# Rounds of four steps in a fused attention kernel, with the side tasks behind the products with V

## What is computed

```python
latent_kv = x @ w_kv_down
kv = latent_kv @ w_kv_up
k, v = (kv[..., :HD], kv[..., HD:])
q = (x @ w_q).reshape(Bx, Tx, N_HEAD, HEAD_SIZE)
att = jnp.einsum('bqhd,bkhd->bhqk', q, k) * scale
att = jnp.where(causal, att, -jnp.inf)
att = jax.nn.softmax(att, axis=-1)
y = jnp.einsum('bhqk,bkhd->bqhd', att, v)
return y.reshape(Bx, Tx, HD) @ w_out
```

## Time and profile before

| | us |
|---|---|
| median of 3 runs | 2115.67 |
| lowest, highest | 2113.73, 2116.21 |
| profiled execution, span from first to last instruction | 2113.7 |
| PE busy | 1984.7 (94%) |
| POOL busy | 1425.9 (67%) |
| DVE busy | 1337.2 (63%) |
| ACT busy | 1097.9 (52%) |

### The profile page before, as it was taken

The page is one execution under the profiler, slowest core; times in us unless marked ns, Lnnn a source line. Parts: engine busy times, 40 slices in busy tenths (PEclk is TensorE's granted clock), DMA queues, the critical chain, the costliest instruction groups (busy, mean ns, idle before and its releaser), DMA issues.

```text
span 2113.7 us, 35206 instructions
## 1 busy us (share of the span) xinstructions
PE 1984.7 (94%) x12886; PEld 1240.9 (59%) x12886; DVE 1337.2 (63%) x2728; ACT 1097.9 (52%) x2236; POOL 1425.9 (67%) x812
## 2 busy tenths in 40 slices
PE   8997788999999999999989999999999999999898
PEld 6775454555655555555555655555555555555466
DVE  7786555576656666666665657576756575656443
ACT  5775543455545454545455444545445445444585
POOL 1333225778687878787857687868786878687822
PEclk9998899999999999999999999999999999999999
DMA  3000000000000000000000000000000000000001
GB/s 124 1 1 1 0 7 13 13 19 10 13 18 16 13 19 12 19 10 19 13 12 17 12 20 11 17 12 20 11 18 11 20 11 18 11 14 11 26 26 60
DMA packets 29243, 37.01 MB, mean 18 GB/s; under 512 B 6928, under 2 KB 20368, under 8 KB 29072
## 3 DMA queue, kind: packets, MB, share of 16 engines
q1 hardware_dynamic: 29072, 34.76, 5.4%
HBM read 30.02 MB, written 4.46 MB: 16 GB/s over the span
## 4 chain that ended last, share of the span: by engine, by line
PE 63%; DVE 14%; POOL 12%; ACT 6%; issue 4%; DMA 1%; POOLq 0%; ACTq 0%; SPq 0%; DVEq 0%
PE heads_out L918 16%; POOL acc L1416 10%; PE beside L723 9%; PE scores L723 7%; PE two_heads L874 7%; PE scores L897 4%; PE scores L903 4%; PE scores L899 4%; PE scores L901 4%; DVE part_max L1112 3%; ACT prob L1331 2%; PE two_heads L723 2%; PE beside L929 2%; PE heads_out L723 1%; DVE wQK_lo L1073 1%
## 5 line engine op out<-in xcount | busy, mean ns | idle before, releaser
L1416 POOL TENSOR_TENSOR acc<-acc,prob 128x1024 f32<-128x1024 f32 (+3 forms) x512 | 1017.9, 1988 | 195.4 <-ACT prob L1331 140.1
L1331 ACT ACTIVATE prob<-scores 128x512 f32<-128x512 f32 (+3 forms) x1280 | 579.4, 539 | 649.2 <-PE scores L903 289.0
L1112 DVE TENSOR_REDUCE part_max<-two_heads 128x2 f32<-128x1024 f32 x384 | 469.3, 1222 | 280.5 <-PE two_heads L874 279.7
L918 PE MATMUL heads_out<-prob,V 128*64 128x512 f32 (+3 forms) x2560 | 544.4, 547 | 0.0
L1109 DVE CUSTOM_DVE_ANT_0 two_heads<-two_heads,mask 128x128 f32<-128x128 f32 (+3 forms) x512 | 242.0, 514 | 180.4 <-PE two_heads L874 180.4
L874 PE MATMUL two_heads<-k_hi,q_hi 64*128 64x512 f32 (+3 forms) x1280 | 274.1, 424 | 62.8 <-DVE part_max L1112 30.6
L918 PEld LDWEIGHTS heads_out<-prob,V 128*64 128x64 f32 x2560 | 156.7, 137 | 232.4 <-issue 209.6
L874 PEld LDWEIGHTS two_heads<-k_hi,q_hi 64*128 64x128 f32 x1280 | 120.6, 184 | 256.6 <-issue 133.4
L897 PE MATMUL scores<-q_hi,k_hi 64*128 64x512 f32 (+3 forms) x1280 | 236.1, 364 | 0.8 <-DVE k_lo L1100 0.5
L903 PE MATMUL scores<-neg_max,sel 64*128 64x512 f32 (+3 forms) x1280 | 235.6, 362 | 0.0
L901 PE MATMUL scores<-q_lo,k_hi 64*128 64x512 f32 (+3 forms) x1280 | 235.5, 362 | 0.0
(11 more groups left out here) (301 smaller groups left out, 2898.7 us busy)
## 6 DMA issues: line engine op xcount, KB each, us to landing
rden<-rden_rows SPq DMA_DIRECT2D x128, 128.0 KB, 2.9
X<-u SPq DMA_DIRECT2D x8, 512.0 KB, 8.7
out<-X SPq DMA_DIRECT2D x8, 512.0 KB, 2.9
wQK_raw<-wQuery SPq DMA_DIRECT2D x16, 192.0 KB, 3.1
wO_raw<-wOut SPq DMA_DIRECT2D x16, 128.0 KB, 2.8
wV_raw<-wValue SPq DMA_DIRECT2D x8, 128.0 KB, 2.9
den<-den_rows SPq DMA_DIRECT2D x64, 4.0 KB
rden_rows<-den SPq DMA_DIRECT2D x64, 4.0 KB, 1.3
```

The source lines that it names most:

```text
L918: made = pe.matmul(heads_out[head(h), x0:], V[vn % NVS][:, tt, p % 2, head(h)], prob[step % NPROB][:, h, x0:], start=t == 0, stop=t == TPB ...
L1112: made = ve.reduce_max(part_max[:, t, :, c:c + 1], two_heads[:, :, 0:width], AX.X)
L1331: ac.activation(prob[step % NPROB][:, h, x0:], bank(task, h)[:, x0:], ACT.Exp).then_inc(empty(task, h)[0], 1)
L1416: po.tensor_tensor(total[:, :, x0:], total[:, :, x0:], new[:, :, x0:], ALU.add).then_inc(acc_ok, 1)
```

## The change

A round now has four steps. Its order is: a maximum, the scores of two steps, a maximum (or a piece of weights), `invert`, the scores of the other two steps, the rest of the round's maxima (one in banks 5 and 6, the next in 0 and 1, a third in 2 and 3), then the products with V of these same four steps with `two_parts` behind the second, and behind them `scale_out`, `denominators` and up to four tasks beside, in banks 7, 3, 2 and 1, the fourth only if it is due within eight steps. The table `TILE` sets in which order a unit takes its key tiles: with j = 3, each round takes three full tiles and one diagonal one; with j = 2 one, one and two; with j = 1 two and two; with j = 0 all four are diagonal. The two heads of a step share one wait, one semaphore and one exponential of up to 1024 columns. Due times of values and of the output's tasks move with the rounds. Nothing is computed that was not before.

```diff
+SIDE = [7, 3, 2, 1]
+TILE = [[0, 1, 2, 3], [0, 1, 4, 5, 2, 3, 6, 7], [0, 1, 2, 8, 3, 4, 5, 9, 6, 7, 10, 11], [0, 1, 2, 12, 3, 4, 5, 13, 6, 7, 8, 14, 9, 10, 11, 15]]
...
+def tile_of(idx, t):
+
+    return TILE[UNITS[idx][2]][t]
+
+
+def left_of(idx, t):
+
+    return P * max(0, tile_of(idx, t) - TPB * UNITS[idx][2])
...
         elif kind == "maximum":
-            self.take(task, (5, 6))
+            self.take(task, (self.max_bank, self.max_bank + 1))
         elif kind == "score":
             n = 2 * (self.step_of[task[1:]] % 2)
-            if task[2] >= TPB * UNITS[task[1]][2]:
+            if tile_of(*task[1:]) >= TPB * UNITS[task[1]][2]:
                 self.masked[task[1:]] = len(self.masked) + 1
-            self.take(task, (n,), (n + 1,))
+            self.take(task, (n, n + 1))
...
             _, idx, t = task
-            x0 = P * max(0, t - TPB * UNITS[idx][2])
+            x0 = left_of(idx, t)
...
-                    out.append((max(start[first] + 2 if j else start[first] - LEAD - 8, at + TPB * j - 14), at + TPB * j - 2 + half, ("value", self.value_of(b, p, j), half)))
+                    out.append((start[first] + 4 * (j - 1) if j else start[first] - LEAD - 8, at - 4 + half, ("value", self.value_of(b, p, j), half)))
...
-        ahead = {-14: [("channel_start", "b"), ("mixer_weights", "b"), ("turn_normal", "b", 0)],
-                 -12: [("turn", "b", 0), ("turn_normal", "b", 1)], -10: [("turn", "b", 1), ("mix_tokens", "b", 0)],
-                 -4: [("turn_normal", "b", 2)], 0: [("mix_tokens", "b", 1)]}
+        ahead = {-16: [("channel_start", "b"), ("mixer_weights", "b"), ("turn_normal", "b", 0)],
+                 -12: [("turn", "b", 0), ("turn_normal", "b", 1)], -8: [("turn", "b", 1), ("mix_tokens", "b", 0)],
+                 -4: [("turn_normal", "b", 2), ("mix_tokens", "b", 1)]}
...
-            later.extend([(s + 2, ("denominators", idx)), (s + 6, ("invert", idx)), (s + 8, ("scale_out", idx)), (s + 10, ("two_parts", idx))])
+            later.extend([(s + 4, ("denominators", idx)), (s + 8, ("invert", idx)), (s + 8, ("scale_out", idx)), (s + 12, ("two_parts", idx))])
...
-        for s in range(0, len(steps) + 2, 2):
+        for s in range(0, len(steps), 4):
             self.in_steps = True
-            if s == 2:
-                self.heads_free = self.freed[4]
...
-            goal = min(len(self.maxima), max(urgent, min(s + 2 + LEAD, self.at + 3))) if self.layers_done else urgent
+            goal = min(len(self.maxima), max(urgent, min(s + 4 + LEAD, self.at + 5))) if self.layers_done else urgent
             if self.at < goal:
                 maximum()
-            due("invert")
             for step in steps[s:s + 2]:
                 self.need("score", *step)
+            if not s:
+                self.in_steps = False
+                yield
+                self.in_steps = True
             if self.at < goal:
                 maximum()
             else:
                 chore()
-            filler(10 ** 6)
-            diagonal = not steps[s:s + 2] or any(t >= TPB * UNITS[idx][2] for idx, t in steps[s:s + 2])
-            if not diagonal:
-                self.side_bank = 0
-                filler(s + 8)
-                self.side_bank = 7
-            while self.at < goal - 1:
+            due("invert")
+            for step in steps[s + 2:s + 4]:
+                self.need("score", *step)
+            self.max_bank = 5
+            while self.at < goal:
                 maximum()
-            for idx, t in steps[max(0, s - 2):s]:
+                self.max_bank = (5, 0, 2)[(5, 0, 2).index(self.max_bank) - 2]
+            self.max_bank = 5
+            if not s:
+                self.heads_free = self.freed[4]
+            for idx, t in steps[s:s + 4]:
                 self.need("weigh", idx, t)
                 self.need("accumulate", idx, t)
+                if (idx, t) == steps[s + 1]:
+                    due("two_parts")
                 if t == TPB * (UNITS[idx][2] + 1) - 1:
                     self.need("take_out", idx)
                     output(idx)
-            if self.at < goal:
-                maximum()
-            due("two_parts")
             due("scale_out")
-            if not due("denominators") and diagonal:
-                filler(s + 8)
+            for n, self.side_bank in enumerate(SIDE):
+                if n or not due("denominators"):
+                    filler(10 ** 6 if n < 3 else s + 8)
+            self.side_bank = 7
             if side:
-                self.add_all(side.pop(0))
+                for piece in (side.pop(0), side.pop(0) if side else []):
+                    self.add_all(piece)
             self.add_all(ahead.get(s - len(steps), []))
             self.in_steps = False
             yield
+        s = len(steps)
...
+        def pair_of(task):
+            first = plan.bank[task][0][0][0]
+            return two_heads if first == 5 else scores[:, first:first + 2, :]
...
-                    for h in range(2):
-                        for s, v in free(task, h):
-                            w.wait_ge(s, v)
+                    for s, v in free(task):
+                        w.wait_ge(s, v)
+                    first = plan.bank[task][0][0][0]
...
                     for h in range(2):
-                        pe.matmul(bank(task, h)[:, x0:], k_hi[g][head(h), kc], q_hi[i][head(h), x0:], start=True, stop=False)
+                        pe.matmul(scores[:, first + h, x0:], k_hi[g][head(h), kc], q_hi[i][head(h), x0:], start=True, stop=False)
...
                     for h in range(2):
-                        pe.matmul(bank(task, h)[:, x0:], sel[head(h), :], neg_max[idx % NMAX][head(h), x0:], start=False, stop=True).then_inc(full(task, h)[0], 1)
+                        made = pe.matmul(scores[:, first + h, x0:], sel[head(h), :], neg_max[idx % NMAX][head(h), x0:], start=False, stop=True)
+                    made.then_inc(full(task)[0], 1)
...
-                    if t >= TPB * UNITS[idx][2]:
+                    if task[1:] in plan.masked:
                         w.wait_ge(masked, plan.masked[idx, t])
-                    for h in range(2):
-                        w.wait_ge(*full(task, h))
-                        ac.activation(prob[step % NPROB][:, h, x0:], bank(task, h)[:, x0:], ACT.Exp).then_inc(empty(task, h)[0], 1)
+                    first = plan.bank[task][0][0][0]
+                    w.wait_ge(*full(task))
+                    ac.activation(prob[step % NPROB][:, :, x0:], scores[:, first:first + 2, x0:], ACT.Exp).then_inc(empty(task)[0], 1)
                 elif kind == "take_out":
...
```

More of the change, by code:

```diff
@@ L873, in tensor_program @@
                     for h in range(2):
-                        made = pe.matmul(two_heads[:, h, 0:width], q[head(h), t * P:(t + 1) * P], k[head(h), 0:width], start=True, stop=True)
+                        made = pe.matmul(pair_of(task)[:, h, 0:width], q[head(h), t * P:(t + 1) * P], k[head(h), 0:width], start=True, stop=True)
                     made.then_inc(full(task)[0], 1)
@@ L1297, in scalar_program @@
                     if idx >= NQ:
-                        w.wait_ge(*full(("score", *last_step(idx - NQ)), 1))
+                        w.wait_ge(*full(("score", *last_step(idx - NQ))))
                     ac.activation(q_hi[idx % NQ][:, :], bank(task), ACT.Copy, scale=DH ** -0.5).then_inc(q_hi_ok, 1)
@@ L1303, in scalar_program @@
                     if idx >= NKS:
-                        w.wait_ge(*full(("score", *last_of_pair(idx - NKS)), 1))
+                        w.wait_ge(*full(("score", *last_of_pair(idx - NKS))))
                     ac.activation(k_hi[idx % NKS][:, :], bank(task), ACT.Copy).then_inc(k_hi_ok, 1)
@@ L1314, in scalar_program @@
                     if idx >= NMAX:
-                        w.wait_ge(*full(("score", *last_step(idx - NMAX)), 1))
+                        w.wait_ge(*full(("score", *last_step(idx - NMAX))))
                     ac.activation(neg_max[idx % NMAX][:, :], bank(task), ACT.Copy, scale=-1.0).then_inc(empty(task)[0], 1)
@@ L1402, in gpsimd_program @@
                     step = step_of[idx, t]
-                    x0 = P * max(0, t - TPB * UNITS[idx][2])
+                    x0 = left_of(idx, t)
                     total, new = acc[idx % 2], prob[step % NPROB]
-                    for h in range(2):
-                        w.wait_ge(*empty(("score", idx, t), h))
+                    w.wait_ge(*empty(("score", idx, t)))
                     if t == 1:
```

25 lines of the change are left out of this document (11 added, 14 removed).

## The result

The changed kernel takes 2311.39 us (median of 4 runs, 2307.58 to 2313.4), the kernel before 2114.7 in the same comparison: 1.0925 times as long (95% interval 1.0909 to 1.0940), 197 us more. The forecast was 2207, range 2075 to 2265: the right side, but 91 us in place of 197.

A forecast was written before the change was run, and what follows sets the result against it. PE, 96% busy in the attention stretch, was taken as the bound. 127 + 16 + 28 + 6 - 74 - 12 = +91 us on the 2113.7 span gives 2204.7; with 2.0 for the median, 2207 us, range 2075 to 2265.

The forecast's parts named there:

- The release time: Score banks: free 1.36 us after their score slot ends, from 0.28 latency, 1.02 merged exponential and 0.06 semaphore.
- M4: Last maximum of a round of four, in the banks of S2: waits 0.11 to 0.64 us with j = 3.
- S2: Third score step of a round, reusing the first one's banks: waits 0.11 us, about 1.0 with j = 0.
- 127 + 16 + 6: PE's costs: 127 us waiting for reused score banks, 16 for `invert` delaying limits, 6 for a fifth maximum in bank 2.
- Tasks beside right ahead of the scores: Tasks in banks 7, 3, 2, 1 before the next round's first scores: their evacuations cost 28 us, bounds 0 and 70.
- What was to be won: PE's waits of maxima for DVE reductions and of denominators for their bank: 74 us, nearly all to go.
- Blocks of four products with V: Weighing in fours instead of twos saves a switch of task kind each round: 12 us won, 0 to 22.
- The faster case: Rival: score banks come free in time, release about 0.9 us, 86 us won, about 2060 us; chance 0.20.
- POOL was no bound: Rival: POOL bounds full-width stretches and spreading diagonal tiles frees it, some 2000 us; chance 0.03, within the faster case's.

The follow-up runs named there:

- b_side_first: Kernel before, with the task beside put ahead of the second maximum in rounds whose two tiles are 256 and 128 wide: 2105.8 us, 0.9951 of before.
- a_tiles_in_order: Changed kernel with each unit's key tiles in natural order, so all four diagonal tiles fall in its last round: 2352.6 us, 1.1134 of before.
- a_late_between: Changed kernel with the fourth maximum behind the second product with V and one task beside between the pairs of scores: 2188.14 us, 1.0351 of before.
- a_max_late: Changed kernel with maxima from the fourth of a round on issued behind the second product with V: 2235.35 us, 1.0579 of before.
- a_dve_clear: Changed kernel with the reciprocal and the maxima's pieces of weights moved behind the second pair of scores: 2263.13 us, 1.0712 of before.
- a_keep_clock: Changed kernel with seven useless transposes between third and fourth maximum in rounds with two or more diagonal tiles: 2307.35 us, 1.0920 of before.
- a_three: Changed kernel with late fourth maximum, reciprocal and weights behind the second scores, and one task beside between the pairs of scores: 2243.37 us, 1.0602 of before.

## Why the prediction was right and wrong

*The release time was right.* ACTIVATE by width in the changed kernel (mean ns after the comma):

```profile
L1352 ACT ACTIVATE prob<-scores 128x1024 f32<-128x1024 f32 x436 | 435.8, 1025 | 325.7 <-PE scores L925 247.2 <-DVE scores L1143 69.9 <-POOL acc L1436 6.6
...
L1352 ACT ACTIVATE prob<-scores 128x768 f32<-128x768 f32 x62 | 50.1, 809 | 8.1 <-DVE scores L1143 4.8 <-POOL acc L1436 3.4
...
L1352 ACT ACTIVATE prob<-scores 128x512 f32<-128x512 f32 x61 | 36.5, 598 | 56.9 <-DVE scores L1143 56.8
...
L1352 ACT ACTIVATE prob<-scores 128x256 f32<-128x256 f32 x61 | 23.3, 382 | 4.5 <-DVE scores L1143 2.5 <-POOL acc L1436 1.5
```

1025 ns at 1024 columns, against 1.02 us forecast. In the four rounds of a unit with j = 3, M4 starts 1.35 to 1.47 us after the slot of S2 ends (forecast 1.36) and loses 0.04, 0.34, 0.49 and 0.66 us in the median (forecast 0.11, 0.33, 0.56, 0.64). M4 costs 97 us by the starts, some fifth maxima included, and the scores 52; the forecast had 127 + 16 + 6 for all of them and `invert`. The sum of 149 is met, its inside only in part, and that is luck: M4 in the last round of j = 2 loses 0.35 in place of 0.8, and in the last round of j = 1 it loses 2.4 in place of 0.8 and half a us for `invert`. The prediction counts `invert` on DVE and leaves out `chore`, the piece of weights that rides with each maximum and stands ahead of the same limits, held up by POOL: of a task that is moved, every rider moves with it.

*Tasks beside right ahead of the scores* were forecast at 28 and cost 32.

*What was to be won failed.* "Nearly all go" of 74 us: 45 did, and 29 us of waits for reductions stayed. This is one step that failed; the other is that three costs had no term at all (below). The forecast counts the distance between two maxima on PE; what it leaves out is what DVE has still to do before it can reduce the first one. In the changed kernel that is a piece of the output's weights (`wO_lo`, issued ahead of the round's first maximum) in 14 waits with 17 us, row statistics of a coming layer in 7 more with 6, and the evacuation of a key in 16 with 5. The reciprocal and the limits have under 1 us of it. In the kernel before, more distance did help wherever there was a task to give it (b_side_first); I had read a releaser as the whole cause.

*Three costs had no term in the sum.* The half clock: 33 us more of it than before. The forecast has PE waiting for over 140 us and treats each wait as its length. The query that is made in the last round before its maxima: 26 us. The tasks of the second sequence (`turn_tiles` and `latent`), now one behind the other behind the products with V: some 13 us more by the starts.

*Blocks of four products with V* were forecast at -12. The step from one weigh task to the next is in fact shorter in the block (0.86 us against 0.91 for full width), the step from a maximum into the block costs 0.1 more than the step from a maximum to a score. By the starts that makes -10 to -20 in all, so I let -12 stand.

Together: 149 + 32 + 33 + 26 + 13 - 45 - 12 = 196, and the spans differ by 192.5 (2306.2 and 2113.7). The forecast had 91: of the 105 between them, 29 are what wasn't won, 33, 26 and 13 the terms left out, and 4 the tasks beside. That is closer than it deserves, since the half clock also stretches the distances that the other terms are read from.

*The rivals.* The faster case needed a release of 0.9 us or less in place of 1.36; nothing of it came. POOL was no bound: its share of the chain fell to 1% while PE's waits grew. It isn't out of the picture either, since it holds the pieces of weights on DVE. (That PE's idle rows of the kernel before name POOL nowhere is almost right: there is one wait of 3.3 us before `project`.) Spreading the tiles does help (41 us), by way of DVE and ACT. The forecast's range ended at 2265, since it allowed for a bad case only of the terms it had.

*Open* is what POOL's hold on the pieces of weights is worth by itself, and whether a kernel with rounds of four and a shorter lead of the maxima could match the one before. The best of them stands 3.5% above it.

## What to carry over

When a bank's turn is shortened from a round to two slots, the chain behind it (last product, limit on DVE, exponential, semaphore) has to be set against the slots of PE that follow, width by width; the time of that chain can be read from the old trace to a few per cent. Then go through every engine of that chain for what is queued ahead of the evacuating instruction, riders included, for it is the round where two small things coincide that costs most. Work that is put off comes in with the first task that needs it, so look where that one stands. And a wait that one releaser ends isn't won by giving it more time, when that releaser is late for its own reasons.

## What the hardware showed that was not expected

PE's granted clock fell to half (1.2 GHz) for some us at a time, mostly behind PE's longest waits: 17 of the changed kernel's 23 low stretches have one of 1.7 to 2.6 us just before them, five have shorter ones or none, and one is the program's end. From 320 us on, the kernel before has 28 us at half clock in 6 stretches, the changed kernel 93 in 23, a_tiles_in_order 160 in 30, a_late_between 39 in 7. In the round shown above a wait of 2.3 us cost another 1.7 us in this way. The Trainium skill (Perfetto Trace Analysis, Matmul Optimizations) says that the matmul engine scales its power with its use, and that matmuls should run back to back in batches. The runs show the clock and not the power: it was at half for 45 us in a_max_late and 48 in a_dve_clear, which took the longest waits away, and a_keep_clock shows that filling the wait with idle transposes only breaks even.

A subtraction on DVE with both operands in SBUF (`wQK_lo`, `wO_lo`) took 0.27 to 0.50 us in some places and up to 2.6 in others. From 320 us on, in the kernel before, the changed kernel, a_three and a_dve_clear, each one over 0.5 us ended 0.15 us (128 columns) or 0.28 us (256) after an operation on POOL ended. The reductions from PSUM kept their 1.2 us beside the same adds on POOL.

Merging two exponentials of 512 columns into one of 1024, with their semaphores and waits, saved 47 us where PE waited for the end of them, and 3 us where it didn't.
